# A perceiver block on one core: the softmax shift of the scores by VectorE instead of by two matmuls, and the context's high part by GpSimd

## What is computed

```python
def reference(x, ctx, ...):                     # x (32, 64, 256), ctx (32, 1601, 256)
    q, k, v = LN(x) @ W_Q + b_Q, ctx @ W_K + b_K, ctx @ W_V + b_V   # 16 heads of 16
    scores = einsum('bhld,bhsd->bhls', q, k) / sqrt(16)
    x = x + einsum('bhls,bhsd->bhld', softmax(scores), v) @ W_O + b_O
    x = x + ssm(LN(x))
    return x + experts(LN(x))
```

## Time and profile before

| | |
|---|---|
| three runs | 2362.01, 2363.89 and 2364.93 us, median 2363.89 |
| the profiled execution | 2363.51 us, its span 2361.8 us |
| PE busy | 2154.9 us, 91% of the span |
| DVE busy | 1444.9 us, 61% |
| ACT busy | 1239.7 us, 52% |
| POOL busy | 797.4 us, 34% |
| mean granted TensorE clock | 0.956 |

### The profile page before, as it was taken

The page is one execution under the profiler, slowest core; times in us unless marked ns, Lnnn a source line. Parts: engine busy times, 40 slices in busy tenths (PEclk is TensorE's granted clock), DMA queues, the critical chain, the costliest instruction groups (busy, mean ns, idle before and its releaser), DMA issues. The chain is left out here.

```text
span 2361.8 us, 65032 instructions
## 1 busy us (share of the span) xinstructions
PE 2154.9 (91%) x28672; PEld 1768.7 (75%) x28672; DVE 1444.9 (61%) x2610; ACT 1239.7 (52%) x1667; POOL 797.4 (34%) x571
## 2 busy tenths in 40 slices
PE   5999999999999999999999997896799997499993
PEld 3789999999999999999999995643233336499993
DVE  4655556555555555565555552427588875688885
ACT  2355555555555555555555553363799971255661
POOL 2222222222222222222222212012699962255551
PEclk8999999999999999999999998987899998699997
DMA  2111111111111111111111103004875521466663
GB/s 90 36 49 46 40 48 39 47 42 39 47 42 40 51 42 41 48 39 47 41 39 48 43 16 103 4 5 185 216 173 145 143 81 55 158 223 224 223 221 123
DMA packets 130685, 197.40 MB, mean 84 GB/s; under 512 B 17714, under 2 KB 108850, under 8 KB 130243
## 3 DMA queue, kind: packets, MB, share of 16 engines
q1 hardware_dynamic: 120594, 176.58, 24.9%
q0 software_dynamic: 4416, 12.06, 1.5%
q10 hardware_dynamic: 5392, 4.59, 0.6%
HBM read 161.60 MB, written 31.59 MB: 82 GB/s over the span
## 5 line engine op out<-in xcount | busy, mean ns | idle before, releaser
L507 DVE TENSOR_REDUCE max_part<-work 128x1 f32<-128x384 f32 (+1 forms) x1024 | 539.2, 570 | 239.7 <-PE work L635 216.2
L570 ACT ACTIVATE probs<-scores 128x1024 f32<-128x1024 f32 (+1 forms) x416 | 423.8, 1026 | 397.5 <-PE scores L660 381.5
L467 POOL TENSOR_TENSOR ctx_lo<-ctx_whole,ctx_hi 128x768 fp32r<-128x768 f32 (+1 forms) x128 | 232.3, 1815 | 1034.2 <-DVE ctx_hi L490 1034.2
L502 DVE SCALAR_TENSOR_TENSOR keys_lo<-work,bk,keys_hi 128x384 fp32r<-128x384 f32 (+1 forms) x256 | 162.6, 636 | 262.2 <-ACT keys_hi L549 262.2
L1193 POOL TENSOR_TENSOR decay<-steps_in,xn 128x1024 f32<-128x1024 f32 x126 | 243.2, 1965 | 53.4 <-DMA steps_in<-scratch_results 39.7
L625 PE MATMUL work<-wv_hi,ctx_hi 128*128 128x256 f32 (+1 forms) x832 | 243.9, 293 | 2.1
L654 PE MATMUL scores<-q_hi,keys_hi 64*128 64x256 f32 (+1 forms) x1664 | 241.9, 283 | 0.0
L654 PE MATMUL scores<-q_lo,keys_hi 64*128 64x256 f32 (+1 forms) x1664 | 237.2, 277 | 0.0
L654 PE MATMUL scores<-q_hi,keys_lo 64*128 64x256 f32 (+1 forms) x1664 | 237.1, 277 | 0.0
L625 PE MATMUL work<-wv_hi,ctx_lo 128*128 128x256 f32 (+1 forms) x832 | 234.4, 282 | 0.0
L674 PE MATMUL acc<-probs,values 128*17 128x64 f32 x13312 | 230.5, 220 | 4.0 <-ACT probs L570 4.0
(11 more groups left out here) (234 smaller groups left out, 4685.4 us busy)
## 6 DMA issues: line engine op xcount, KB each, us to landing
xs<-in_w_T SPq DMA_DIRECT2D x46, 1024.0 KB
ctx_whole<-in_ctx_T SPq DMA_DIRECT2D x96, 384.0 KB, 3.2
steps_in<-scratch_results SPq DMA_DIRECT2D x256, 128.0 KB, 2.7
ctx_whole<-in_ctx_T SPq DMA_DIRECT2D x32, 449.0 KB, 3.5
scratch_results<-steps SPq DMA_DIRECT2D x16, 512.0 KB, 2.6
scratch_mixed<-mixed ACTq DMA_DIRECT2D x32, 128.0 KB, 1.7
mixed_b<-scratch_mixed SPq DMA_DIRECT2D x4, 1024.0 KB, 13.6
scratch_z<-z SPq DMA_DIRECT2D x16, 256.0 KB, 2.5
```

What stands on the lines that cost most here:

```text
L467: nc.gpsimd.tensor_tensor(ctx_lo[c][:, :, 0:n], s.ctx_whole[c % 2][:, :, 0:n], ctx_hi[c][:, :, 0:n].bitcast(F32), ALU.subtract).then_inc(l ...
L502: nc.vector.scalar_tensor_tensor(keys_lo[par][:, m, start:start + n], bank[:, 0:n], s.bk[:, m:m + 1], keys_hi[par][:, m, start:start + n]. ...
L507: nc.vector.reduce_max(max_part[par][:, place(pair), c:c + 1], bank[:, 0:CHUNKS[c][1]], AX) \
L570: nc.scalar.activation(probs[slot][0:rows, :], scores[slot][0:rows, :], ACT.Exp, scale=1.0 / HD ** 0.5).then_inc(exp_done, 1)
```

## The change

It does four things in the attention, and none in the other layers:
- The two matmuls L660 are gone from every tile. The sums of the twelve L654 are complete by themselves.
- Two units `wide` are added at the end of a batch's list, which now has 51. They multiply ones by `shifts` once, with 512 columns each, so that the shift stands on all 128 rows. ScalarE copies them to `wide0` or `wide1` in SBUF.
- VectorE adds `wide` to the scores of every tile, in place in PSUM (`shift`), between the maxima. The exponential waits for that addition, no longer for the matmuls. VectorE's order is now written by passes as TensorE's is.
- From the second batch on GpSimd makes `ctx_hi` too, by a multiplication with one, ahead of its `ctx_lo`. VectorE makes it for the first batch alone.

The diff, cut to its core:

```diff
@@ -351,9 +351,15 @@
 ]
-UNITS = [unit for tiles, before, after in PAIRS_OF_TILES for unit in sum(before, []) + after]
+LAST_UNITS = [("wide", 0), ("wide", 1)]
+UNITS = [unit for tiles, before, after in PAIRS_OF_TILES for unit in sum(before, []) + after] + LAST_UNITS
+SHIFTED = list(range(NT))
+NS = len(SHIFTED)
 NU = len(UNITS)
 ROW = UNITS.index(("row",))
+WIDE = [UNITS.index(unit) for unit in LAST_UNITS]
 LAST_MAX = max(u for u in range(NU) if UNITS[u][0] == "max")
@@ -369,7 +375,7 @@
                      or (UNITS[u][0] == "k" and UNITS[u][2] == c)) for c in range(len(CHUNKS))]
-COPIED_KINDS = ("v",)
+COPIED_KINDS = ("v", "wide")
 CREDIT = 2
@@ -395,6 +401,7 @@
         shifts = sb("shifts", [P, BANK], F32R)
+        wide = [sb(f"wide{i}", [P, HEADS * LATENTS]) for i in range(2)]
         ones = sb("ones_row", [P, P], F32R)
@@ -413,6 +420,7 @@
         shift_made = sem("shift_made")
+        shifted = sem("scores_shifted")
         exp_done = sem("exp_done")
@@ -463,6 +471,12 @@
                 n = even(CHUNKS[c][1])
+                if b >= 1:
+                    pool.wait_ge(s.ctx_loaded[c % 2], (b * (NC // 2) + c // 2 + 1) * 16)
+                    pool.wait_ge(unit_done, (b - 1) * NU + LAST_OF_CHUNK[c] + 1)
+                    nc.gpsimd.tensor_tensor(ctx_hi[c][:, :, 0:n], s.ctx_whole[c % 2][:, :, 0:n],
+                                            s.one[:, :].rearrange("p (a b) -> p a b", a=1).to_broadcast([P, KD, n]),
+                                            ALU.mult).then_inc(hi_split, 1)
                 pool.wait_ge(hi_split, b * NC + c + 1)
@@ -482,13 +496,10 @@
         def _(dve):
-            def split(b, c):
+            def split_first(c):
                 n = even(CHUNKS[c][1])
-                dve.wait_ge(s.ctx_loaded[c % 2], (b * (NC // 2) + c // 2 + 1) * 16)
-                if not isinstance(b, int) or b >= 1:
-                    dve.wait_ge(unit_done, (b - 1) * NU + LAST_OF_CHUNK[c] + 1)
-                nc.vector.tensor_copy(ctx_hi[c][:, :, 0:n], s.ctx_whole[c % 2][:, :, 0:n]) \
-                    .then_inc(hi_split, 1)
+                dve.wait_ge(s.ctx_loaded[c % 2], (c // 2 + 1) * 16)
+                nc.vector.tensor_copy(ctx_hi[c][:, :, 0:n], s.ctx_whole[c % 2][:, :, 0:n]).then_inc(hi_split, 1)
@@ -520,12 +531,31 @@
-            def prepare(b, par, more=True):
-                for u in range(NU):
+            def shift(b, par, t):
+                n = b * NT + t
+                rows = TILES[t][1]
+                bank = scores[(par * NT + t) % 2]
+                dve.wait_ge(scores_ready, n + 1)
+                if t == SHIFTED[0]:
+                    wait_evacuated(dve, b, WIDE[1])
+                nc.vector.tensor_tensor(bank[0:rows, :], bank[0:rows, :], wide[par][0:rows, :], ALU.add) \
+                    .then_inc(shifted, 1)
+            def prepare(b, par, units):
+                for u in units:
                     if UNITS[u][0] not in COPIED_KINDS:
                         unit(b, par, u)
-                    if more and u in LAST_OF_CHUNK:
-                        split(b + 1, LAST_OF_CHUNK.index(u))
+            def attend(b, par, ahead):
+                for tiles, before, after in BESIDE:
+                    for t, units in zip(tiles, before):
+                        if ahead:
+                            prepare(b + 1, 1 - par, units)
+                        if t in SHIFTED:
+                            shift(b, par, t)
+                    if ahead:
+                        prepare(b + 1, 1 - par, after)
@@ -533,10 +563,10 @@
             for c in range(NC):
-                split(0, c)
-            prepare(0, 0)
-            for b in range(1, batches):
-                prepare(b, b % 2, more=b + 1 < batches)
+                split_first(c)
+            prepare(0, 0, range(NU))
+            for b in range(batches):
+                attend(b, b % 2, b + 1 < batches)
@@ -558,6 +588,12 @@
                         .then_inc(unit_copied, 1)
+                elif UNITS[u][0] == "wide":
+                    h = UNITS[u][1]
+                    act.wait_ge(unit_done, b * NU + u + 1)
+                    if b >= 2:
+                        act.wait_ge(shifted, (b - 1) * NS)
+                    nc.scalar.copy(wide[par][:, h * BANK:(h + 1) * BANK], bank[:, :]).then_inc(unit_copied, 1)
@@ -565,13 +601,19 @@
                         rows = TILES[t][1]
-                        act.wait_ge(scores_ready, n + 1)
+                        if t in SHIFTED:
+                            act.wait_ge(shifted, b * NS + SHIFTED.index(t) + 1)
+                        else:
+                            act.wait_ge(scores_ready, n + 1)
                         act.wait_ge(probs_used, n + 1)
...
                             unit(b + 1, 1 - par, u)
+                if ahead:
+                    for u in WIDE:
+                        unit(b + 1, 1 - par, u)
                 act.wait_ge(probs_used, b * NT + NT + CREDIT)
@@ -635,6 +677,10 @@
                                             start=True, stop=True)
+                elif kind == "wide":
+                    h = UNITS[u][1]
+                    wait_evacuated(pe, b, ROW)
+                    last = nc.tensor.matmul(bank[:, :], ones[side(h), :], shifts[side(h), :], start=True, stop=True)
                 else:
@@ -652,13 +698,13 @@
                             last = nc.tensor.matmul(bank[0:rows, at:at + GCOLS], k[par][side(g), m, start:start + rows],
-                                                    q[par][side(g), m, :], start=(m == 0 and n == 0), stop=False,
+                                                    q[par][side(g), m, :], start=(m == 0 and n == 0),
+                                                    stop=(t in SHIFTED and m == KD - 1 and n == len(parts) - 1),
                                                     skip_group_check=True)
-                if t == 0:
-                    wait_evacuated(pe, b, ROW)
-                for h in range(2):
-                    last = nc.tensor.matmul(bank[0:rows, h * BANK:(h + 1) * BANK], ones[side(h), 0:rows],
-                                            shifts[side(h), :], start=False, stop=True, skip_group_check=True)
+                if t not in SHIFTED:
+                    for h in range(2):
+                        last = nc.tensor.matmul(bank[0:rows, h * BANK:(h + 1) * BANK], ones[side(h), 0:rows],
+                                                shifts[side(h), :], start=False, stop=True, skip_group_check=True)
                 last.then_inc(scores_ready, 1)
@@ -689,6 +735,9 @@
                         mix(b, par, t)
+                if ahead:
+                    for u in WIDE:
+                        unit(b + 1, 1 - par, u)```

On VectorE, the order around passes 0 and 1 of a batch in the middle. Before:

```order
L502 SCALAR_TENSOR_TENSOR keys_lo<-work,bk,keys_hi 128x384 x2
L507 TENSOR_REDUCE max_part<-work 128x1 x6
L502 SCALAR_TENSOR_TENSOR keys_lo<-work,bk,keys_hi 128x384 x2
L490 CAST ctx_hi<-ctx_whole 128x768
L507 TENSOR_REDUCE max_part<-work 128x1 x6
```

## The result

The changed kernel takes 2627.6 us in the median (2623.8 to 2629.7, four runs) beside 2363.6 of the kernel before: a ratio of 1.112, 95% interval 1.110 to 1.114. It is 264 us slower. 2605 was forecast, with 2560 to 2700 around it.

What follows compares the result with a forecast made beforehand. TensorE alone bounded the attention; VectorE's additions would make it wait through three work banks. 2363.5 + 231 (31 batches x 7.46) + 8 (last batch) + 1.5 (first `wide`) = 2604, say 2605 us, range 2560 to 2700.

Steps and rivals of the forecast that it cites:

- The bound of the batch: Attention: VectorE's additions delay the maxima that free three work banks, TensorE waits in order behind: +7.46 us a batch.
- the walk: Step-by-step timing of passes 0 to 6 from trace durations: 50.65 us a batch, 2604 us in all; chance 0.67.
- a fresh start: Pass 1, second key unit: 0.17 us from VectorE freeing the bank to TensorE's start, chosen between 0 and 0.28.
- The addition: VectorE's 128x1024 addition in PSUM, thirteen a batch, priced from the scan's row at 1.23 us each.
- Steps shorter than durations: VectorE's list: the next instruction starts 0.09 us before the last ends, stepping 0.46 per maximum, 1.14 per addition.
- The rival by whole durations: VectorE's instructions start only when the last is done: batch 52.9 us, 2674 us in all; chance 0.12.
- GpSimd: Its casts, priced as subtractions at 1.70 and 2.15 us, leave masked queries ready 0.7 us before the first maximum.
- the last batch: Last batch, without units: two tiles go from 3.7 to about 5.0 us, 8 us more in all.
- the clock: TensorE's granted clock in the attention was taken as 1.00, as before the change.
- the rival at 0.91: TensorE, busy some 80% of a batch in pieces, drops to clock 0.91: 2730 us; chance 0.08.
- The fourth rival: Additions short enough for the banks, below some 0.4 us: TensorE bounds the batch at 40.4 us, 2282 us; chance 0.05.
- a term that did not matter here: Attention: removing thirteen pairs of shift matmuls a batch takes 13 x 0.23 = 3.0 us off TensorE.

Runs made afterwards that it cites:

- Idle reductions: Changed kernel, but matmuls add the shift again and VectorE, at the additions' places, reduces an unused SBUF tile nobody waits for: 2587.4 us, ratio 1.093.
- half width: Changed kernel, but VectorE adds the shift to only 512 of the 1024 columns, 0.69 us an addition: 2444.1 us, ratio 1.033.
- additions alone: Changed kernel with the casts of the context back on VectorE at their old places: 2631.3 us, ratio 1.112.
- narrow run: Changed kernel, but VectorE adds the shift to only 64 of the 1024 columns, all waits kept, 0.22 us an addition: 2363.1 us, ratio 0.999.
- No shift at all: Kernel before, with the two shift matmuls of each tile left out and nothing in their place: 2317.5 us, ratio 0.980.
- kernel with additions and zero matmuls: Changed kernel, with two matmuls of 512 columns by zeros put back on every tile: 2628.2 us, ratio 1.111.
- idle additions: Changed kernel, but matmuls add the shift again and VectorE, at the additions' places, adds an unused SBUF tile to itself: 2761.8 us, ratio 1.168.

## Why the prediction was right, point by point

- **The bound of the batch.** That TensorE's list would stand behind VectorE's through the three work banks was the mechanism, and the walk gave passes 1 to 6 to a tenth of a microsecond and pass 0 to 0.2: passes 0 to 6 were put at 6.40, 8.17, 8.87, 8.34, 7.12, 6.65 and 5.10 us and took 6.59, 8.15, 8.90, 8.36, 7.15, 6.68 and 5.03. The sum, 50.65, came out as 50.86. Idle reductions and half width show it as a cause, not only as a fit. The 0.17 us that were chosen for a fresh start came out as 0.05 ahead of the second key unit and 0.11 in its first step (0.46 instead of 0.35). In pass 0 the copies of `wide` ended after 1.27 us and not 1.0, and the last keys, for which the next pass waits, were ready at 6.44 instead of 6.33.
- **The addition.** 1.23 us from the scan's row against 1.22.
- **Steps shorter than durations.** The next instruction of VectorE started 0.09 us before the end of the last: 660.95 + 1.22 - 662.08. The rival by whole durations, 2674, did not come about for instructions with nothing to wait for. The section that the prediction cites from the Trainium skill, "VectorE: DVE Perf Modes", The DRAIN you can't avoid, says more than the sentence taken from it: it adds that a next instruction that is not held starts earlier, and the trace agrees with that.
- **GpSimd.** The cast took 1.69 us for the last chunk instead of the 2.15 I took for the subtraction. The queries were masked 1.3 us before the first maximum (658.26 to 659.56). They hold nothing.
- **Mis-sized, the last batch.** 8 us were put for it and it took 16.2. I walked it at full clock; its granted clock was 0.73 over 1677 to 1718 us, where the kernel before had 1.00 with 84% of TensorE busy. The run with the additions alone tells the two apart: in its last batch two pairs of tiles ran at 1.00 and took 5.06 us each, where the walk had 5.0, the others at 0.64 to 0.78 and took 5.5 to 6.2. Six such steps took 35.9 us in the changed kernel; at 5.06 each they would be 30.4, so that by this estimate 5.5 us are the clock's. Another 2.9 lie ahead of the first exponential, where the copies of `wide` stand and the forecast had 1.5.
- **Mis-sized, the clock.** The forecast set it at 1.00 for all batches and the rival at 0.91. It was neither: at 1.00 except for one short fall in seven of the 31 batches, which take 52.35 instead of 50.85 us. That is 7 x 1.5 = 10.5 us. With 31 x 0.21 = 6.5 for the walk, less 0.8 in a shorter first cycle, and 8 for the last batch this makes 24, about what lies between 2605 and 2628.
- **Wrong, what shorter additions would give.** The fourth rival counted on 2 us for each us of an addition in each of passes 1 to 4 and 3 in pass 5. From 1.22 to 0.69 us it was 2.0 in passes 1 and 2, 1.7 and 1.4 in 3 and 4, and 1.3 in pass 5. Half width should have left 50.65 - 12 x 0.54 = 44.2 us a batch and left 45.56, and the narrow run, for which the rival had 40.4, took 43.0.
- **Wrong, a term that did not matter here.** "Thirteen pairs of shift matmuls a batch, 13 x 0.23 = 3.0 us of TensorE" stood there as time to be had, in the 40.4 us of a batch and so in the 2282 us of the fourth rival. No shift at all shows 1.5 us. A busy share of 99.8% (43.12 of 43.19 us) did not mean that TensorE's work alone set the pass: VectorE's taking out of the banks was just hidden behind it.

## What to carry to other kernels

When an engine gets new work, read in its list what is queued behind that work and which buffers this releases, and walk one period in durations from the trace; sums of busy time gave a gain here of 2.8 us a batch where the lists gave a loss of 7.5. Work that is added among the instructions that free a short ring of buffers costs even if nobody waits for its result: here about half of its duration, 6.4 us for ten pieces of 1.21 us, and from 0.69 us on the whole of each further microsecond in passes 1 and 2 and 0.6 to 0.85 of it in passes 3 to 5. Before counting on time that is taken off the busiest engine, look for the next wait that this work covers, and take it out once with nothing in its place.

## What the runs showed of the hardware

**TensorE's clock fell in single short stretches.** In the changed kernel such falls lie at 252, 508, 716, 920, 1176, 1380 and 1584 us, four or five batches apart. One of them by stretch: a granted clock of 0.59 over 4 us means that most of it was at the lower of the two levels, 1.2 GHz.

```profile
716.00:720.00 4.00, 4.00 (x76) 3.73 (x74) 1.25 (x3) 1.57 (x4) 0.86 (x1) 0.59 0.00 0
```

TensorE's timeline there: the pairs of key matmuls step by 0.35 us ahead of the fall and by 0.63 in it. The engine had waited 0.91 us for VectorE ahead of 713.54 and 0.28 at 715.60. Waits of these lengths come in every batch.

```profile
714.46 0.52 PE L657 MATMUL work<-ctx_lo,wk_hi 128*128 128x384 f32 x2
714.81 0.51 PE L657 MATMUL work<-ctx_hi,wk_lo 128*128 128x384 f32 x2
715.60 0.83 PE L657 MATMUL work<-ctx_hi,wk_hi 128*128 128x384 f32 x2 [0.28 <-DVE max_part L518]
716.23 0.84 PE L657 MATMUL work<-ctx_lo,wk_hi 128*128 128x384 f32 x2
```

Over 100 to 1650 us TensorE was busy for 1342 of 1550 us there. The kernel with additions and zero matmuls is busy for 1419 us in the same stretch, waits at most 0.6 us for a maximum (650 to 1150 us) instead of 1.0, and shows no fall. The changed kernel's row:

```profile
100.00:1650.00 1550.00, 1342.16 (x22218) 1154.15 (x22221) 1109.78 (x1667) 683.83 (x1000) 497.26 (x390) 0.99 0.13 36
```

The row of the kernel with both:

```profile
100.00:1650.00 1550.00, 1419.28 (x23043) 1203.70 (x23042) 1114.61 (x1671) 687.88 (x1002) 499.02 (x390) 1.00 0.13 36
```

The additions alone have eight batches with a fall. The idle additions have one or two in nearly every batch, a mean of 0.96 over 100 to 1800 us, though TensorE is busy there for 1484 of 1700 us, the same share as in the changed kernel; its single waits are longer, up to 1.4 us behind a maximum instead of 1.0. So the busy share alone does not tell. The Trainium skill describes such a swing for short idle times between groups of matmuls ("TensorE: Matmul & The Clock Gate", A second HAM failure mode: psum-queue depth-cycling); this case's runs agree that such falls occur beside short waits, and size them at 10.5 of 2628 us. That the waits cause them is not shown, and why one batch and not the next stays open: no run here moved the waits alone. The last batch, at 0.73, may be of the same kind; there TensorE was busy for 26.9 of 41 us.

**VectorE and GpSimd disturb each other when VectorE has two operands in SBUF.** Such an addition (a tile with itself) took 1.21 us alone and up to 3.07 beside GpSimd, GpSimd's last subtraction 3.01 us instead of 2.14. With one operand in PSUM (the changed kernel, 1.218 to 1.233 us over 416 additions, 122 of them beside a subtraction of GpSimd) or with a single operand in SBUF (the reductions) there was nothing of it. The Trainium skill names the case ("GPSIMD Engine Reference", Specifications: contention with two SBUF inputs) and the trace agrees.
